# Ten shared-expert tiles lead instead of eight, TensorE adds the expert rows of six token tiles in PSUM, and ten tiles' gated results are prepared between routed tiles

## The chip, the cores and the metric

The kernel runs on one core of a Trainium2 chip. The metric is the device time of one execution in microseconds. The engines are TensorE (PE; its weight loads are PEld), VectorE (DVE), ScalarE (ACT), GpSimd (POOL) and SyncE (SP), which here only issues transfers.

## The reference

One transformer block over x of 8 batches x 256 tokens x 256 values, fp32, with adaptive layer norm. `sa, ca, ga, sb, cb, gb` are six rows per batch from a small product of the condition.

```python
h = layernorm(x) * (1 + ca) + sa
x = x + ga * attention(h)        # 8 heads, 2 kv heads, window of 64, softcap 30
h = layernorm(x) * (1 + cb) + sb
x = x + gb * moe(h)
# moe: 16 experts, each token goes to 4 of them (from 2 of 4 groups), weights normalised
y = sum over the token's 4 experts of weight * ((silu(h @ w1[e]) * (h @ w3[e])) @ w2[e])
z = (silu(h @ sw1) * (h @ sw3)) @ sw2          # two shared experts of 176
moe = y + z
```

The change concerns only the last line of the block, x + gb * (y + z), and the order in which z and y are computed.

## The kernel before, in words

**Tiles and units.** The 2048 tokens are 16 token tiles of 128. After attention, every token's row (256 values, its weights and its target ids) is sent by GpSimd to the slots of its four experts in device memory (`rows_d`, 64 indirect transfers). The expert part is a list of 96 jobs: shared tiles 0 to 7, then 80 routed tiles of 128 slots each (16 experts, partly padded), then shared tiles 8 to 15. A shared tile is two units (two shared experts), a routed tile one: 112 units, numbered from 0; routed units are 16 to 95. `FIRST` is the number of shared tiles that lead.

**Steps.** Each engine has its own written order, one function `step(u)` per unit. In step u, TensorE transposes the rows of the tile that starts with unit u+2, multiplies unit u up (`up_mm`, L1640 to L1642, from fp32 split into a high and a low part, three products each), turns the hidden rows of unit u-2 and multiplies unit u-3 down (L1662 to L1666) into one of two PSUM banks for results (`y_bank`). ScalarE makes high parts and silu, and in step u evacuates the result of the job that ended with unit u-4: for a shared tile into `hrow` (L1452, over the tile's own input, so it waits until the tile's rows are sent), for a routed tile into `yout` (L1456), from where GpSimd sends the rows to `y_d`, four rows to a token (L1422). VectorE makes low parts (L1548, L1577) and the product of silu and up part (`hidden`, L1570, L1573). The low part of expert n's weights is split off by VectorE in unit `HIGH_AT[n] + 1` (L234, L241), every second unit.

**The first ten steps** of the expert part are woven by hand into the end of attention and routing (`drain`). There the last rows are sent and the table of routed tiles is worked out; SyncE then issues the loads of slot rows (`xin`, L1402), six tiles ahead, each released by the `hidden` of six tiles before.

**The tail.** SyncE issues behind the last `xin` the eight rows `gb` (one for each batch, spread over 128 partitions, L1406), waits until all of `y_d` is written, and loads for each token tile its four rows per token (`yt`, 512 KB, L1411) and x1, the block's x before the experts (`x1t`, four tiles at a time, L1413). GpSimd adds the four rows in two operations for each of 16 tiles (L1426, L1428). VectorE's `combine(t)` adds the shared result in `hrow` (L1486), multiplies by gb (L1489), adds x1 (L1492); SyncE stores the tile (L1388). `combine(0)` stands in step 103, one more in each step behind it, the last three behind the steps.

## Time and profile before

| | us |
|---|---|
| median of 3 runs | 536.2 (529.27 to 537.77) |
| profiled execution | 530.26 |
| its span | 528.4 |
| TensorE busy | 412.7 |
| VectorE busy | 384.7 |
| GpSimd busy | 259.2 |
| ScalarE busy | 243.5 |
| moved by DMA | 69.69 MB, mean 132 GB/s |

The span is the time from the first to the last instruction of the profiled execution; 1.9 us lie around it. Busy times are sums over stretches with different work: attention up to about 250 us, routed tiles from 299.5 to 472, the tail behind them. A row of the timeline gives start and length of an instruction, or of several alike, and in brackets how long its engine had been idle and what released it. "issue" is a wait for nothing that the profile shows; "remote" is one whose releaser is not among the core's own recorded events.

### The profile page before, as it was taken

The page shows a single profiled execution, that of the slowest core. Times are in us where ns is not written, and L with a number is a line of the kernel's source. Part 1 is how long each engine was busy: PE and PEld are TensorE (multiplying, and loading weights), DVE is VectorE, ACT ScalarE, POOL GpSimd, SP SyncE. Part 2 cuts the span into 40 slices and gives each one's busy share as a digit, 9 for nine tenths or more (in the row PEclk, how much of TensorE's full clock was granted, in tenths as well). Part 3 has the DMA queues.
Part 4 walks back from the last instruction along what each step waited for, and adds up shares of the span by engine and source line. Part 5 has one row for each costly group of instructions (what it writes and reads, how often), then busy time and mean ns, then how long its engine had stood idle before and what let it go on. Part 6 is the DMA issues. An engine that isn't in the chain of part 4 may idle for free.

```text
span 528.4 us, 10590 instructions
## 1 busy us (share of the span) xinstructions
PE 412.7 (78%) x2841; PEld 376.0 (71%) x2841; DVE 384.7 (73%) x1175; ACT 243.5 (46%) x569; POOL 259.2 (49%) x262
## 2 busy tenths in 40 slices
PE   3758869778967666097834999999999999998543
PEld 3447768676856554096734988999999999988532
DVE  2698796986867773228756889877777777747997
ACT  3446647434461501123322777566666666644210
POOL 1294262434867577404374026544545444446990
PEclk9855997877998855559795999999999999999875
DMA  8422313301230309202352636444444444639932
GB/s 304 154 70 88 96 37 108 99 0 62 66 110 20 122 31 334 88 0 86 128 222 72 205 101 198 139 140 147 139 142 139 138 143 139 152 103 345 396 125 90
DMA packets 38712, 69.69 MB, mean 132 GB/s; under 512 B 5753, under 2 KB 27897, under 8 KB 38657
## 3 DMA queue, kind: packets, MB, share of 16 engines
q1 hardware_dynamic: 30736, 45.51, 27.2%
q0 software_dynamic: 6912, 19.93, 10.2%
q10 hardware_dynamic: 1008, 3.57, 2.2%
q8 instruction: 27, 0.44, 0.4%
q14 instruction: 29, 0.23, 0.1%
HBM read 42.49 MB, written 26.51 MB: 131 GB/s over the span
## 4 chain that ended last, share of the span: by engine, by line
PE 46%; DVE 23%; issue 10%; another core or an unknown queue 6%; POOL 6%; ACT 5%; DMA 3%; DVEq 0%; SPq 0%; ACTq 0%; POOLq 0%
PE sc_ps L1640 5%; PE sc_ps L1642 5%; PE sc_ps L1641 5%; PE qkv_ps L1623 3%; POOL rn L449 3%; DVE yt L1486 2%; DVE yt L1489 2%; PE qkv_ps L912 2%; PE pv L1003 2%; PE pv L1004 2%; PE pv L1001 2%; DMA y_d<-yout,to 1%; PE qkv_ps L914 1%; PE qkv_ps L913 1%
## 5 line engine op out<-in xcount | busy, mean ns | idle before, releaser
L1422 POOL DMA_INDIRECT y_d<-yout,to x80 | 81.2, 1015 | 108.8 <-ACT yout L1456 102.3
L1291 POOL DMA_INDIRECT rows_d<-hrow,slots x64 | 67.5, 1054 | 36.9 <-issue 16.8
L449 POOL TENSOR_TENSOR rn<-meansq,minus_half 128x12 f32<-128x12 f32 x16 | 36.7, 2306 | 64.4 <-DVE meansq L710 64.4
L1570 DVE SCALAR_TENSOR_TENSOR hid<-silu,xin,sc_ps 128x64 f32<-128x64 f32 (+1 forms) x160 | 47.2, 336 | 20.5 <-PE tp L1651 7.2
L1435 ACT ACTIVATE f_xh<-qkv_ps 128x256 fp32r<-128x256 f32 x96 | 36.9, 384 | 52.2 <-PE qkv_ps L1623 42.4
L1640 PE MATMUL sc_ps<-w_routed,f_xh 128*128 x160 | 58.3, 365 | 0.0
L1440 ACT ACTIVATE silu<-sc_ps 128x176 f32<-128x176 f32 x112 | 35.7, 319 | 47.7 <-PE sc_ps L1642 40.2
L1642 PE MATMUL sc_ps<-w_routed,f_xh 128*128 x160 | 51.7, 323 | 0.0
L1641 PE MATMUL sc_ps<-w_routed,f_xl 128*128 x160 | 51.6, 323 | 0.0
L1548 DVE TENSOR_TENSOR f_xl<-qkv_ps,f_xh 128x256 fp32r<-128x256 f32 x96 | 40.6, 423 | 12.0 <-ACT f_xh L1435 7.5
L1623 PE MATMUL qkv_ps<-ident,xin 128*128 128x128 f32 x160 | 30.6, 273 | 0.2 <-DMA xin<-rows_d 0.2
L1640 PEld LDWEIGHTS sc_ps<-w_routed,f_xh 128*128 128x128 f32 x160 | 30.2, 189 | 0.5 <-issue 0.2
L1641 PEld LDWEIGHTS sc_ps<-w_routed,f_xl 128*128 128x128 f32 x160 | 30.4, 190 | 0.0
L973 PE MATMUL sc_ps<-mask,ident_b 128*128 128x320 bf16 x64 | 15.7, 384 | 18.4 <-ACT capped L551 18.1
L1642 PEld LDWEIGHTS sc_ps<-w_routed,f_xh 128*128 128x128 f32 x160 | 30.0, 188 | 0.0
L551 ACT ACTIVATE capped<-sc_ps 128x1280 f32<-128x1280 f32 x16 | 19.8, 1240 | 21.8 <-remote 16.7
L1003 PE MATMUL pv<-v,probs 128*128 128x33 f32 x128 | 27.6, 300 | 0.0
L1004 PE MATMUL pv<-v,probs 128*128 128x33 f32 x128 | 27.6, 300 | 0.0
L1573 DVE TENSOR_TENSOR hid<-silu,sc_ps 128x64 f32<-128x64 f32 x64 | 14.8, 272 | 16.9 <-ACT silu L1440 10.7
L1445 ACT ACTIVATE f_hth<-sc_ps 128x256 fp32r<-128x256 f32 x59 | 22.8, 387 | 8.8 <-PE sc_ps L1651 3.4
L1426 POOL TENSOR_TENSOR yt<-yt 128x512 f32<-128x512 f32 x16 | 22.1, 1380 | 5.8 <-DMA yt<-y_d 5.8
L1577 DVE TENSOR_TENSOR f_htl<-sc_ps,f_hth 128x256 fp32r<-128x256 f32 x59 | 24.6, 417 | 0.0
(261 smaller groups left out, 1371.1 us busy)
## 6 DMA issues: line engine op xcount, KB each, us to landing
xin<-rows_d SPq DMA_DIRECT2D x80, 144.0 KB
yt<-y_d SPq DMA_DIRECT2D x16, 512.0 KB, 11.6
raw<-in_w_raw SPq DMA_DIRECT2D x9, 608.0 KB
mod<-mod_rows SPq DMA_DIRECT2D x8, 384.0 KB
w_stage<-in_w_raw SPq DMA_DIRECT2D x4, 608.0 KB
raw<-in_w_raw ACTq DMA_DIRECT2D x4, 608.0 KB
rows_d<-zeros SPq DMA_DIRECT2D x16, 144.0 KB
x1d<-x SPq DMA_DIRECT2D x8, 256.0 KB
```

What stands on the lines that cost most here:

```text
L449: pool.tensor_tensor(rn[:, part], meansq[:, part], minus_half[:, part], ALU.pow).then_inc(s.rn_done, 1)
L1003: pe.matmul(o[:, 1, j], probs[:, g, j, 2 * P:3 * P], v[:, p, 0, g], start=True, stop=False, skip_group_check=True)
L1004: mm = pe.matmul(o[:, 1, j], probs[:, g, j, 0:P], v[:, p, 1, g], start=False, stop=True, skip_group_check=True)
L1291: pool.indirect_dma_start(rows_d, bass.IndirectOffsetOnAxis(ap=r.slots[:, t, k:k + 1], axis=0), hrow[:, t], None).then_inc(r.sent[t // QT] ...
L1422: pool.indirect_dma_start(y_d, bass.IndirectOffsetOnAxis(ap=to[:, i:i + 1], axis=0), yout[:, i % YR], None)\
L1435: act.activation(xh[:, j % XB], xt_ps[:], ACT.Copy).then_inc(s.xh, 1)
L1548: dve.tensor_tensor(xl[:, j % XB], xt_ps[:], xh[:, j % XB].bitcast(F32), ALU.subtract).then_inc(s.xl, 1)
L1570: dve.scalar_tensor_tensor(out=hid[:, u % HB3, to_cols], in0=silu[:, u % 2, cols], scalar=weight, in1=y, op0=ALU.mult, op1=ALU.mult).then_ ...
L1623: mm = pe.transpose(xt_ps[:, c], src[:, c * P:(c + 1) * P], ident[:])
L1640: pe.matmul(o, xh[:, j % XB, c], wh, start=(c == 0), stop=False)
L1641: pe.matmul(o, xl[:, j % XB, c], wh, start=False, stop=False)
L1642: mm = pe.matmul(o, xh[:, j % XB, c], wl, start=False, stop=(c == KC - 1))
```

## The change

- `FIRST` is 10: units 0 to 19 are shared, 20 to 99 routed, 100 to 111 shared. The weight splits of experts 7 to 17 stand at unit 10, 12, ... instead of 8, 10, ...
- For the six token tiles 10 to 15, ScalarE no longer evacuates the shared result and GpSimd no longer adds rows. The result stays in PSUM (three banks in turn), and TensorE adds the token's four rows to it, by four products with the identity (`add_rows`, step of the tile's last unit + 5). VectorE's `combine` then has two operations: times gb (read from PSUM), plus x1.
- For the ten leading tiles, `base(t)` runs between routed tiles, in step 42 + 4t: `hrow` = shared result times gb, plus x1, two VectorE operations. x1 comes through one buffer of a tile (`x1b`), its load issued by SyncE ahead of the `xin` load number 24 + 4t. `combine` has two operations here as well: the four rows' sum times gb, plus `hrow`.
- The `gb` rows are loaded ahead of the `xin` load number 20.
- The `yt` loads and the stores follow the order in which VectorE combines: 10, 11, 0, 1, 12, 2, 3, 13, 4, 5, 14, 6, 7, 15, 8, 9, from step 106 to step 117. For tiles 10 to 15 x1 follows each `yt` load.

```diff
-FIRST = 8
+FIRST = 10
-HIGH_AT = {n: 8 + 2 * (n - EARLY) for n in range(EARLY, NE)}
+HIGH_AT = {n: 10 + 2 * (n - EARLY) for n in range(EARLY, NE)}
-            for u in range(10, f.units + 3):
+            for u in range(10, f.units + 5):
...
-    results = [sc_ps[:, 3], qkv_ps[:, 1]]
+    results = [sc_ps[:, 3], qkv_ps[:, 1], pv[:]]
...
     def y_bank(j):
+        if j >= FIRST + TILES:
+            return (j - FIRST - TILES) % 3
         return (j - TWO_Y) % 2 if j >= TWO_Y else 0
...
+    x1b = w.raw[:].rearrange("p a n -> p (a n)")[:, B * HID:(B + 1) * HID]
+    GATES_AT = 20
+    LOAD_X1_AT = {GATES_AT + 4 + 4 * t: t for t in range(FIRST)}
+    BASE_AT = {SHARED * FIRST + i - 2: t for i, t in LOAD_X1_AT.items()}
...
-    COMBINE_AT = SHARED * FIRST + TILES + 7
+    COMBINE_AT = SHARED * FIRST + TILES + 8
+    PUT = {}
+    for t in range(FIRST, NT):
+        PUT.setdefault(last[TILES + t] + 5, []).append(t)
+    for t in range(FIRST):
+        PUT.setdefault(COMBINE_AT + t, []).append(t)
+    ORDER = [t for u in sorted(PUT) for t in PUT[u]]
...
         for i in range(TILES):
             if i >= XR:
                 sp.wait_ge(s.hid, first[FIRST + i - XR] + 1)
+            if i == GATES_AT:
+                for n in (NE - 2, NE - 1):
+                    split_done(sp, w, n)
+                for b in range(B):
+                    sp.dma_start(gb[:, b], mod_rows[b:b + 1, 3].to_broadcast([P, HID])).then_inc(gb_in, 16)
+            if i in LOAD_X1_AT:
+                t = LOAD_X1_AT[i]
+                after(sp, s.based, 2 * t)
+                sp.dma_start(x1b, x1d[t]).then_inc(x1_in, 16)
...
-        for n in (NE - 2, NE - 1):
-            split_done(sp, w, n)
-        for b in range(B):
-            sp.dma_start(gb[:, b], mod_rows[b:b + 1, 3].to_broadcast([P, HID])).then_inc(gb_in, 16)
...
-        for t in range(NT):
+        for t in ORDER:
             rows = y_d[t * P * TOPK:(t + 1) * P * TOPK].rearrange("(p k) h -> p (k h)", k=TOPK)
             sp.dma_start(yt[:, t], rows).then_inc(yt_in[t], 16)
-            if t % 4 == 0:
-                sp.dma_start(x1t[:, t:t + 4], x1d[t:t + 4].rearrange("t p h -> p t h")).then_inc(x1_in[t // 4], 16)
+            if t >= FIRST:
+                sp.dma_start(x1t[:, t], x1d[t]).then_inc(yt_in[t], 16)
...
-        for t in range(NT):
+        for t in range(FIRST):
             pool.wait_ge(yt_in[t], 16)
...
-            if ends(u - 4):
+            if ends(u - 4) and units[u - 4][0] < FIRST + TILES:
                 evacuate(units[u - 4][0])
...
+    def base(dve, t):
+        dve.wait_ge(s.evac, t + 1)
+        dve.wait_ge(gb_in, 16 * B)
+        dve.tensor_tensor(hrow[:, t, 0:HID], hrow[:, t, 0:HID], gb[:, t // QT], ALU.mult).then_inc(s.based, 1)
+        dve.wait_ge(s.based, 2 * t + 1)
+        dve.wait_ge(x1_in, 16 * (t + 1))
+        dve.tensor_tensor(hrow[:, t, 0:HID], hrow[:, t, 0:HID], x1b, ALU.add).then_inc(s.based, 1)
...
     def combine(dve, t):
+        if t < FIRST:
+            dve.wait_ge(s.added2, t + 1)
+            dve.tensor_tensor(yt[:, t, HID:2 * HID], yt[:, t, 0:HID], gb[:, t // QT], ALU.mult).then_inc(s.based, 1)
+            dve.wait_ge(s.based, 2 * FIRST + t + 1)
+            dve.tensor_tensor(x1t[:, t], yt[:, t, HID:2 * HID], hrow[:, t, 0:HID], ALU.add).then_inc(s.stored, 1)
+        else:
+            dve.wait_ge(s.total, t - FIRST + 1)
+            dve.wait_ge(gb_in, 16 * B)
+            dve.tensor_tensor(yt[:, t, HID:2 * HID], results[y_bank(TILES + t)][:, 0:HID], gb[:, t // QT], ALU.mult).then_inc(s.taken, 1)
+            dve.wait_ge(s.taken, t - FIRST + 1)
+            dve.tensor_tensor(x1t[:, t], yt[:, t, HID:2 * HID], x1t[:, t], ALU.add).then_inc(s.stored, 1)
...
             if 0 <= u - 2 < N:
                 low(u - 2)
+            if u in BASE_AT:
+                base(dve, BASE_AT[u])
+            for t in PUT.get(u, []):
+                combine(dve, t)
...
+        def add_rows(t):
+            pe.wait_ge(yt_in[t], 32)
+            o = results[y_bank(TILES + t)][:, 0:HID]
+            for k in range(TOPK):
+                mm = pe.matmul(o, ident[:], yt[:, t, k * HID:(k + 1) * HID], start=False, stop=(k == TOPK - 1))
+            mm.then_inc(s.total, 1)
...
             if 0 <= u - 3 < N:
                 down_mm(u - 3)
+            if ends(u - 5) and units[u - 5][0] >= FIRST + TILES:
+                add_rows(units[u - 5][0] - TILES)
```

## Rows read from the trace of the kernel before

**Rows 1.** Page, part 1: busy time, share of the span, instructions.

```profile
PE 412.7 (78%) x2841; PEld 376.0 (71%) x2841; DVE 384.7 (73%) x1175; ACT 243.5 (46%) x569; POOL 259.2 (49%) x262
```

**Rows 2.** Busy time (count) by stretch, granted clock, DMA share, GB/s.

```profile
299.51:336.89 37.38, 35.05 (x243) 31.95 (x242) 33.35 (x98) 26.06 (x69) 15.68 (x12) 1.00 0.46 138
336.89:463.01 126.12, 126.12 (x946) 124.79 (x945) 94.63 (x314) 78.70 (x249) 59.76 (x63) 1.00 0.48 142
...
482.00:515.40 33.40, 19.27 (x111) 16.62 (x109) 32.85 (x52) 8.11 (x24) 32.11 (x30) 0.84 0.76 287
515.40:528.43 13.03, 4.46 (x17) 3.74 (x17) 10.35 (x27) 1.15 (x3) 0.08 (x1) 0.50 0.26 91
```

**Rows 3.** Who ended TensorE's waits, 262 to 290: total, times, longest.

```profile
PE sc_ps L1662 <- ACT hrow L1452: 12.3, 1, 12.3
```

**Rows 4.** Timeline: start, us, engine, line, [idle before <-releaser], 273 to 296.

```profile
273.73 0.32 ACT L1440 ACTIVATE silu<-sc_ps 128x176 f32<-128x176 f32 x1 [4.37 <-remote]
...
283.63 0.38 ACT L1452 ACTIVATE hrow<-sc_ps 128x256 f32<-128x256 f32 x1 [6.67 <-remote]
...
289.24 30.67 SPq L1402 DMA_DIRECT2D xin<-rows_d  x14
...
295.38 0.38 PE L1623 MATMUL qkv_ps<-ident,xin 128*128 128x128 f32 x2
```

**Rows 5.** Timeline where routed tiles end and loads begin, 472 to 484.

```profile
472.21 0.29 PE L1666 MATMUL sc_ps<-w_routed,f_htl 128*128 x1
...
475.67 0.32 SPq L1411 DMA_DIRECT2D yt<-y_d  x1
...
479.39 1.29 POOL L1426 TENSOR_TENSOR yt<-yt 128x512 f32<-128x512 f32 x1 [5.21 <-DMA yt<-y_d]
...
482.11 1.56 POOL L1426 TENSOR_TENSOR yt<-yt 128x512 f32<-128x512 f32 x1 [0.61 <-DMA yt<-y_d]
```

**Rows 6.** Timeline: a shared unit, a weight split, the gate rows' loads.

```profile
291.75 0.41 PE L1640 MATMUL sc_ps<-w_shared,f_xh 128*128 128x352 f32 x1
...
312.13 1.15 DVE L234 TENSOR_TENSOR w_routed<-raw,w_routed 128x960 fp32r<-128x960 f32 x1
313.31 0.42 DVE L241 TENSOR_TENSOR w_routed<-raw,w_routed 64x256 fp32r<-64x256 f32 x1
...
454.38 3.67 SPq L1406 DMA_DIRECT2D raw<-mod_rows  x8
```

**Rows 7.** Who ended ScalarE's waits, 455 to 475.

```profile
ACT yout L1456 <- DMA y_d<-yout,to: 3.4, 2, 2.2
```

**Rows 8.** Two transfers in the chain that ended last: start, us.

```profile
314.93 5.67 DMA xin<-rows_d
...
458.36 7.61 DMA y_d<-yout,to
```

**Rows 9.** By line, busy us, mean ns: VectorE 482 to 515.4, GpSimd's tail.

```profile
L1492 DVE TENSOR_TENSOR x1t<-yt,x1t 128x256 f32<-128x256 f32 x8 | 10.5, 1308 | 0.3
L1486 DVE TENSOR_TENSOR yt<-yt,hrow 128x256 f32<-128x256 f32 x8 | 9.0, 1131 | 0.0
L1489 DVE TENSOR_TENSOR yt<-yt,raw 128x256 f32<-128x256 f32 x8 | 7.3, 909 | 0.3
...
L1577 DVE TENSOR_TENSOR f_htl<-tp,f_hth 128x256 fp32r<-128x256 f32 x5 | 2.1, 413 | 0.0
...
L1426 POOL TENSOR_TENSOR yt<-yt 128x512 f32<-128x512 f32 x16 | 22.1, 1380 | 5.8 <-DMA yt<-y_d 5.8
L1428 POOL TENSOR_TENSOR yt<-yt 128x256 f32<-128x256 f32 x16 | 12.7, 793 | 1.3
```

**Rows 10.** Groups by line, VectorE behind 515.4.

```profile
L1489 DVE TENSOR_TENSOR yt<-yt,raw 128x256 f32<-128x256 f32 x8 | 3.4, 425 | 0.3
```

**Rows 11.** Timeline: the widest full fp32 products in the trace.

```profile
17.45 3.60 PE L1046 MATMUL sc_ps<-probs,ct_silu 128*8 128x512 f32 x8
```

**Rows 12.** Timeline: the last operation of a computing engine.

```profile
525.87 0.43 DVE L1492 TENSOR_TENSOR x1t<-yt,x1t 128x256 f32<-128x256 f32 x1
```

More of the change, by code:

```diff
@@ L1361, in experts @@
     s = named({n: sem("f_" + n) for n in (
-        "xt xh xl up silu hid dup ht hth htl down evac to summed stored added1 added2 gated spread").split()})
+        "xt xh xl up silu hid dup ht hth htl down evac to total taken based stored added1 added2 spread").split()})
     x_in = [sem(f"f_x_in{j}") for j in range(XR)]
@@ L1384, in ends, with store @@
         return 0 <= u < N and last[units[u][0]] == u
-    def store(sp, c):
-        sp.wait_ge(s.stored, c + 1)
-        sp.dma_start(out[c], x1t[:, c]).then_inc(out_sent, 16)
+    def store(sp, n, t):
+        sp.wait_ge(s.stored, n + 1)
+        sp.dma_start(out[t], x1t[:, t]).then_inc(out_sent, 16)
     def sync(sp):
@@ L1480, in scalar @@
         return step
-    def combine(dve, t):
-        dve.wait_ge(s.added2, t + 1)
-        total = yt[:, t, 0:HID]
-        dve.wait_ge(s.evac, FIRST if t < FIRST else TILES + t + 1)
-        dve.tensor_tensor(total, total, hrow[:, t, 0:HID], ALU.add).then_inc(s.summed, 1)
-        dve.wait_ge(s.summed, t + 1)
-        dve.wait_ge(gb_in, 16 * B)
-        dve.tensor_tensor(yt[:, t, HID:2 * HID], total, gb[:, t // QT], ALU.mult).then_inc(s.gated, 1)
-        dve.wait_ge(s.gated, t + 1)
-        dve.wait_ge(x1_in[t // 4], 16)
-        dve.tensor_tensor(x1t[:, t], yt[:, t, HID:2 * HID], x1t[:, t], ALU.add).then_inc(s.stored, 1)
+    def base(dve, t):
[5 more added lines that the diff above has]
+        dve.tensor_tensor(hrow[:, t, 0:HID], hrow[:, t, 0:HID], x1b, ALU.add).then_inc(s.based, 1)
+    def combine(dve, t):
+        if t < FIRST:
[9 more added lines that the diff above has]
+            dve.tensor_tensor(x1t[:, t], yt[:, t, HID:2 * HID], x1t[:, t], ALU.add).then_inc(s.stored, 1)
     def finish(dve):
-        for t in range(N + 4 - COMBINE_AT, NT):
-            combine(dve, t)
+        for u in range(N + 4, max(PUT) + 1):
+            for t in PUT.get(u, []):
+                combine(dve, t)
     def place_last(dve):
@@ L1591, in step @@
                 low(u - 2)
-            if 0 <= u - COMBINE_AT < NT:
-                combine(dve, u - COMBINE_AT)
+            if u in BASE_AT:
+                base(dve, BASE_AT[u])
+            for t in PUT.get(u, []):
+                combine(dve, t)
         return step
@@ L1659, in down_mm @@
             if begin:
-                after(pe, s.evac, same_before(y_bank, j))
+                before = same_before(y_bank, j)
+                after(pe, s.evac, min(before, FIRST + TILES))
+                after(pe, s.taken, before - FIRST - TILES)
             o = results[y_bank(j)][:, 0:HID]
@@ L1665, in down_mm @@
             pe.matmul(o, hth[:, q, 1], at(P, O2B, RAW), start=False, stop=False)
-            pe.matmul(o, htl[:, q, 1], at(P, O2B, RAW), start=False, stop=end).then_inc(s.down, 1)
+            pe.matmul(o, htl[:, q, 1], at(P, O2B, RAW), start=False, stop=end and j < FIRST + TILES).then_inc(s.down, 1)
+        def add_rows(t):
[4 more added lines that the diff above has]
+            mm.then_inc(s.total, 1)
         def step(u):
```

6 lines of the change are left out of this document (3 added, 3 removed).

## The prediction, made before the changed kernel ran

> **What bounds the kernel now.** I read the head of the page first, then busy time by stretches, then who ended TensorE's waits, then the order of instructions at the two joints. TensorE is the busiest engine, but its share is an average of very different stretches [rows 1]. While the routed tiles run, it is never idle: 63 units (946 pieces, 15 to a unit) in 126.12 us, 2.00 each. After 482 us VectorE is the full one (32.85 of 33.40 us) and GpSimd runs beside it without a pause, while TensorE drops to 58% and in the last 13 us to the lower clock [rows 2]. So the change has two sides: what it does to the time at which the routed tiles end, and what it does to the tail behind them.
>
> There is a third place. Before the routed tiles TensorE stands for 12.3 us until a ScalarE copy at 283.63. ScalarE itself was waiting, three times in a row (the first and the last are shown), for something that the trace calls remote [rows 3, 4]. I can't name the cause. GpSimd is sending rows all through this stretch, and nothing up to shared unit 9 is changed but a weight split that moves from unit 8 to unit 10. So I keep the wait as it is. The first rows load only at 289.24, and TensorE turns the first routed tile at 295.38, when they are barely there [rows 4]: the eight leading tiles already fill the time until then.
>
> **The routed tiles end later.** Call T0 the issue of the first load of gathered rows, 475.67. It follows the last routed unit's down product (472.21) by a fixed chain: ScalarE's copy, GpSimd's send, its landing [rows 5].
> - Two more tiles lead: four units. Shared units 12 to 15 took from 291.75 to 299.51, where the first routed unit starts, 1.94 each [rows 2, 6]: **+7.8**. Nothing covers them, since TensorE works without a gap from there on.
> - Weight splits. The 16 routed units from 299.51 to 336.89 took 37.38 where 16 x 2.00 is 32.0 [rows 2]. They hold seven splits (1.15 + 0.42 of VectorE each [rows 6]), so a split among routed units costs 0.76, and among shared units nothing, as 1.94 shows. With splits two units and tiles two units later, one more falls among shared units: **-0.8**. The weights stay ahead of their tiles (split 17 at unit 31, used at unit 35).
> - `base`: ten times two VectorE operations of 0.42 [rows 10], 0.87 in one unit of four. VectorE does 94.63 us in 63 units, 1.50 of every 2.00 [rows 2]. A split (1.57) exceeds the spare of two units (1.0) by 0.6 and costs 0.76; `base` doesn't exceed it. Between 0 and 0.16 x 10 = 1.6: **+0.5**. Its x1 load is issued four units (8.0 us) ahead of its use; rows loads on the same queue, with the same lead, cost nothing in the steady stretch.
> - The gate rows' eight loads move from behind the last rows load to ahead of the 21st. Their issue takes 3.67 us and today delays the sends of results, for which ScalarE waits 3.4 us [rows 6, 7]. That price moves along. New is that rows loads stand behind them: 3.67 + a landing of up to 7.61 [rows 8] is 11.3 against 8.0 of lead, so 0 to 3.3. One MB at the 0.4 MB/us of the tail is 2.5, and with about 2.4 of latency the sum is 8.6: **+0.8** with a little delay of results beside it.
> - Third result bank, order of stores, fewer ScalarE copies (six of 0.38 less [rows 4]): 0. ScalarE is busy 8.11 of 33.40 us in the tail [rows 2].
>
> T0 moves by 7.8 - 0.8 + 0.5 + 0.8 = **+8.3**, to 484.0.
>
> **The tail, from T0.** Today it is 528.43 - 475.67 = 52.8 us. GpSimd adds 16 tiles at 1.38 + 0.79 = 2.2 us from 479.39 on [rows 5, 9]. VectorE's three combining operations read two SBUF operands and take 1.31, 1.13 and 0.91 beside GpSimd, against 0.42 when it has stopped [rows 9, 10]. The difference that reads PSUM keeps its 0.41 in the same stretch [rows 9]. So: an operation from two SBUF operands costs 1.1 beside GpSimd, one with a PSUM operand 0.4. All of today's tail is 24 of the first kind, the unit work, and eight combines at the end.
>
> The Trainium skill ("SBUF — State Buffer", section Who interferes with whom) states the same split by operands and that the pair of ports is held for the whole instruction. By that, an operation arriving at random would wait half of a GpSimd operation, about 0.55, and take 0.97 instead of 1.1: the tail would be about 1 us shorter. The rows decide for 1.1.
>
> After the change:
> - Loads. Today the first half MB is used 3.7 us after T0 and the second load, behind 1.5 MB, after 6.4 [rows 5]: 2.4 us and then 0.4 MB/us. New order 10, 11, 0, 1, 12, 2, 3, 13, 4, 5, 14, 6, 7, 15, 8, 9, with x1 rows behind 10 to 15: tile 10 is there at +3.9, tile 0 at +6.8, tile 9 at +25 to +28.
> - GpSimd: ten tiles from +6.8 at 2.2 are done at +29, at the latest +29.7.
> - TensorE. Unit 103 starts 3.3 before T0, as unit 99 does today right behind the down product at 472.21 [rows 5]; a unit takes 1.9. Adding a tile's rows is four full fp32 products of 256 columns. The nearest row is four products of 512 columns that stand as eight pieces, 3.60 us together [rows 11]; half the columns make 1.8 us at the full clock, up to 3.6 at the lower one.
> - VectorE, in its written order. Tile 10: rows added by TensorE at +6.0, stored +6.9. Unit 108 and tiles 11 and 0: TensorE's sum +11.9, VectorE 0.4 + 1.1 + 2.2, to +15.6. Unit 109, tile 1: +18.8. Unit 110, tiles 12 and 2: +23.3. Unit 111, tile 3: +26.5. Tiles 13 and 4: +30.2; GpSimd has stopped. Last difference and tile 5: +31.5. TensorE now does the last down product, the rows of 14 (+33.2) and of 15 (+34.9); VectorE follows with 14, 6, 7, 15, 8, 9 at 0.9 each: **+38.6**. The last store adds 2.1, as today (525.87 + 0.43 against 528.43 [rows 12]): +40.7. For rows that TensorE adds at the lower clock, which it has today in the last 13 us [rows 2], I add 0.8 of the possible 2.3: **41.5**.
>
> The tail loses 52.8 - 41.5 = 11.3, the front gives back 8.3: **-3.0 us**. The profiled execution took 530.3 (span 528.4 and 1.9 around it), so 527.3 of that kind. The median of the runs shown, 536.2, lies 5.9 above the profiled one; with the same difference the changed kernel stands at **533**.
>
> **The rivals.**
> 1. *The tail is bound by GpSimd's ten tiles alone.* If VectorE and TensorE keep up, the end is T0 + 29.7 + 0.9 + 2.1 = 32.7, and the whole -11.8 (524). For: VectorE has 12 + 20 combining operations instead of 48. Against: five operations of 1.1 and 2.4 us of unit work per two units are 7.9, against the 3.8 of TensorE's two units. Chance 0.12.
> 2. *The two tiles cost little in front,* because the 12.3 us wait is shorter in other executions or under this order. Without it unit 10 could start at about 274 and the first routed tile would stand waiting for rows until 295; two more tiles would fill that. The front would then give back some 2 and the total be -9 (527), up to -12. Against: the wait is in the execution that is the second fastest of four. Chance 0.12.
> 3. *Slower: `base` waits for its x1 rows.* The wait stands on VectorE between a difference and the next unit's product, so all of the pipeline stands behind it. It decides once the load takes over 8.0 us. A rows load took 5.67 and a send of results beside the gate loads 7.61 [rows 8]. To reach +2% (10.7 us) the ten must cost (10.7 + 3.0) / 10 = 1.4 each, a landing of 9.4; at 10 us the total is +17 (553). Against: in the steady stretch no rows load was late. Chance 0.06.
> 4. *The tail does not shorten,* since VectorE ends up waiting for TensorE, which waits for loads and for VectorE in turn, at the lower clock: sums of 3.6 us put the last of them 5 to 8 us later, and the total is +2 to +5 (540). Chance 0.12.
>
> **How the numbers follow.** The forecast has 0.58, its own range -9 to +2. A measurement of this kernel can tell about 2% (10.7 us) from no change. Faster by more: most of rival 1, some of rival 2, a corner of the forecast: 0.22. Slower by more: rival 3 and a corner of 4: 0.08. Same: 0.70. The runs before spread from 529.3 to 537.8 by themselves; with the bounds of 1 (-12) and 4 (+5) around 533 the range is 522 to 541.
>
> **What would show it.** Right: unit 99 at the place where unit 95 was plus 8; first load of rows at about 484; two-operand operations of 1.1 until GpSimd stops about 29 us later, PSUM-reading multiplications of 0.4; eight pieces of 1.8 us per tile on TensorE. Wrong: no 12 us wait ahead of unit 9's products; idle VectorE in the tail; VectorE waiting for x1 in the routed stretch; TensorE's rows waiting for a load.

## The result

The changed kernel takes **541.9 us** (median of six runs, 537.1 to 546.1), the kernel before 536.9 in the same comparison (six runs, 529.3 to 629.8). Some executions of either kernel are slower than the rest, and the ratios and their 95% intervals, here and below, are worked out without them. The ratio is 1.0136 (1.0087 to 1.0186): about 7 us slower, under the 2% that a measurement of this kernel can tell from no change. The prediction was 533, its range 522 to 541.

The profiled execution took 546.1 us and has a span of 543.2. First the busy times, which answer to [rows 1], then the same stretches of both kernels. In a row of windows stand the stretch, its length, and then for each engine busy time and count; behind them are the granted clock, the DMA share and GB/s.

The kernel after, page, part 1:

```profile
PE 431.2 (79%) x2889; PEld 388.8 (72%) x2889; DVE 376.3 (69%) x1179; ACT 243.0 (45%) x563; POOL 245.5 (45%) x250
```

The kernel before: the first 23 routed units, the next 47, and the last routed and first shared units up to the start of unit 99:

```profile
299.51:350.91 51.40, 49.07 (x348) 45.83 (x347) 43.95 (x133) 34.91 (x97) 22.33 (x19) 1.00 0.46 139
350.91:445.11 94.20, 94.20 (x708) 93.20 (x707) 70.76 (x236) 59.37 (x188) 44.90 (x48) 1.00 0.46 141
445.11:472.33 27.22, 25.98 (x192) 25.25 (x191) 17.72 (x61) 15.52 (x50) 12.43 (x14) 1.00 0.50 135
```

The kernel after: the same units (numbers four higher), and the tail from the start of unit 103, which answers to the last two of [rows 2]:

```profile
313.83:371.37 57.54, 50.75 (x348) 48.18 (x347) 42.27 (x131) 34.04 (x96) 21.45 (x19) 0.94 0.46 139
371.37:472.87 101.50, 101.24 (x709) 93.31 (x707) 76.60 (x256) 60.66 (x188) 45.62 (x48) 1.00 0.47 144
472.87:498.34 25.47, 25.47 (x192) 25.20 (x190) 17.64 (x61) 15.87 (x50) 12.26 (x14) 1.00 0.31 98
498.34:543.20 44.86, 30.18 (x192) 27.66 (x190) 30.50 (x66) 7.74 (x24) 22.66 (x22) 0.94 0.70 258
```

Unit 10 starts at 286.4 before and at 293.9 after; of what was changed only the place of one weight split lies ahead of it, and 6.1 of the 7.5 us are there at unit 0 already, so I set them aside. From there on:

| | before | after | difference | predicted |
|---|---|---|---|---|
| unit 10 to the first routed unit | 13.1 | 19.9 | +6.8 | +7.8 |
| 23 routed units | 51.4 | 57.5 | **+6.1** | 0 (gate loads +0.8, a split -0.8) |
| the next 47 | 94.2 | 101.5 | **+7.3** | +0.5 |
| up to unit 99 (103) | 27.2 | 25.5 | -1.8 | 0 |
| from there to the end | 56.1 | 44.9 | -11.2 | -11.3 |

From unit 10 to the end that is +7.3 us, as much as the ratio says. The match is no proof of the parts: the two profiled executions lie 15.8 us apart (546.1 and 530.3), and half of that is the 7.5 us ahead of unit 10. The tail came out as forecast, the two more tiles nearly so. The loss lies in two stretches that I had priced at next to nothing. The -1.8 belongs to the gate loads too: they have left that place. With these loads behind the last rows load the stretch takes 26.1 to 27.2 us (e4, e2 and the kernel before), in all fifteen profiles with them ahead of it 25.5.

**The first 23 routed units.** Timeline of the kernel after around them: SyncE's issues, GpSimd's sends of results, and TensorE.

```profile
344.35 2.71 SPq L1426 DMA_DIRECT2D xin<-rows_d  x2
348.37 5.21 SPq L1419 DMA_DIRECT2D raw<-mod_rows  x8
...
353.26 0.96 POOL L1442 DMA_INDIRECT y_d<-yout,to  x1 [1.04 <-ACT yout L1476]
354.07 3.08 SPq L1426 DMA_DIRECT2D xin<-rows_d  x4
...
358.67 0.69 PE L1655 MATMUL qkv_ps<-ident,xin 128*128 128x128 f32 x2 [4.61 <-DMA xin<-rows_d]
359.09 0.65 PE L1672 MATMUL sc_ps<-w_routed,f_xh 128*128 x1
...
360.33 0.96 POOL L1442 DMA_INDIRECT y_d<-yout,to  x1 [6.11 <-ACT yout L1476]
```

The eight gate rows' loads hold the queue for 5.2 us and bring 1 MB ahead of the next rows. TensorE stands 4.6 us for them, and its next products run at the lower clock (L1672 takes 0.65 there and 0.42 at the full clock, below; the granted clock of the whole stretch is 0.94). The three units around it took 7.05, 3.69 and 2.58 instead of 2.0 each: +7.3.

**The next 47.** No wait of TensorE stands in this stretch: it counts as busy for 101.24 of 101.50 us, yet does the same 47 units as before in 94.20. The cause is seen only in the order of instructions. VectorE, then TensorE, around one `base`:

```profile
388.71 0.42 DVE L1607 TENSOR_TENSOR f_htl<-sc_ps,f_hth 128x256 fp32r<-128x256 f32 x1
389.05 0.41 DVE L1505 TENSOR_TENSOR hrow<-hrow,raw 128x256 f32<-128x256 f32 x1
389.50 0.42 DVE L1508 TENSOR_TENSOR hrow<-hrow,raw 128x256 f32<-128x256 f32 x1
389.84 0.42 DVE L1578 TENSOR_TENSOR f_xl<-qkv_ps,f_xh 128x256 fp32r<-128x256 f32 x1
...
390.40 0.41 PE L1655 MATMUL qkv_ps<-ident,xin 128*128 128x128 f32 x2
390.84 0.42 PE L1672 MATMUL sc_ps<-w_routed,f_xh 128*128 x1
```

`f_xl` (L1578) is the difference that frees the one PSUM bank of turned rows. In a unit without `base` ahead of it, it starts 0.7 us after the unit's first product; here it starts 1.34 us after it (the unit's first product was at 388.50). TensorE turns the next rows (L1655) only behind it, and the next unit starts after 2.34 instead of 2.00. That is +0.34 for a `base`, and the unit behind it is late too (2.15).

### The profile page after: what moved, and what is told of

The parts are those of the page before. It is cut to its first block, busy times and chain, and to the rows that moved or that the text cites. A ratio compares the mean times of both kernels' runs of the same rounds, so it can differ in the third digit from the quotient of the medians.

```text
span 543.2 us, 10664 instructions
## 1 busy us (share of the span) xinstructions
PE 431.2 (79%) x2889; PEld 388.8 (72%) x2889; DVE 376.3 (69%) x1179; ACT 243.0 (45%) x563; POOL 245.5 (45%) x250
## 4 chain that ended last, share of the span: by engine, by line
PE 55%; DVE 15%; issue 10%; another core or an unknown queue 6%; ACT 5%; POOL 4%; DMA 2%; SPq 1%; DVEq 0%; ACTq 0%
PE sc_ps L1672 6%; PE sc_ps L1674 5%; PE sc_ps L1673 5%; PE qkv_ps L1655 4%; POOL rn L449 3%; PE qkv_ps L912 2%; PE sc_ps L1696 2%; PE sc_ps L973 1%; PE qkv_ps L913 1%; PE qkv_ps L914 1%; PE pv L1004 1%; PE pv L1003 1%; PE pv L1001 1%; PE qkv_ps L1696 1%
## 5 line engine op out<-in xcount | busy, mean ns | idle before, releaser
L1600 DVE SCALAR_TENSOR_TENSOR hid<-silu,xin,sc_ps 128x64 f32<-128x64 f32 (+1 forms) x160 | 47.1, 335 | 24.5 <-issue 11.2
L1455 ACT ACTIVATE f_xh<-qkv_ps 128x256 fp32r<-128x256 f32 x96 | 36.8, 384 | 58.2 <-PE qkv_ps L1655 36.2
L1672 PE MATMUL sc_ps<-w_routed,f_xh 128*128 x160 | 59.5, 372 | 0.3
L1578 DVE TENSOR_TENSOR f_xl<-qkv_ps,f_xh 128x256 fp32r<-128x256 f32 x96 | 40.6, 423 | 21.2 <-ACT f_xh L1455 18.4
L1674 PE MATMUL sc_ps<-w_routed,f_xh 128*128 x160 | 52.2, 326 | 0.0
L1655 PE MATMUL qkv_ps<-ident,xin 128*128 128x128 f32 x160 | 31.2, 277 | 4.6 <-DMA xin<-rows_d 4.6
L1672 PEld LDWEIGHTS sc_ps<-w_routed,f_xh 128*128 128x128 f32 x160 | 30.6, 191 | 2.7 <-issue 1.8
L973 PE MATMUL sc_ps<-mask,ident_b 128*128 128x320 bf16 x64 | 16.3, 395 | 19.8 <-ACT capped L551 19.1
L1004 PE MATMUL pv<-v,probs 128*128 128x33 f32 x128 | 28.5, 308 | 0.0
L1003 PE MATMUL pv<-v,probs 128*128 128x33 f32 x128 | 28.5, 308 | 0.0
L1603 DVE TENSOR_TENSOR hid<-silu,sc_ps 128x64 f32<-128x64 f32 x64 | 14.9, 274 | 19.0 <-ACT silu L1460 12.6
L973 PEld LDWEIGHTS sc_ps<-mask,ident_b 128*128 128x128 bf16 x64 | 7.3, 126 | 25.2 <-ACT capped L551 21.4
```

The lines of the kernel that those rows point to most:

```text
L1003: pe.matmul(o[:, 1, j], probs[:, g, j, 2 * P:3 * P], v[:, p, 0, g], start=True, stop=False, skip_group_check=True)
L1455: act.activation(xh[:, j % XB], xt_ps[:], ACT.Copy).then_inc(s.xh, 1)
L1578: dve.tensor_tensor(xl[:, j % XB], xt_ps[:], xh[:, j % XB].bitcast(F32), ALU.subtract).then_inc(s.xl, 1)
L1600: dve.scalar_tensor_tensor(out=hid[:, u % HB3, to_cols], in0=silu[:, u % 2, cols], scalar=weight, in1=y, op0=ALU.mult, op1=ALU.mult).then_ ...
L1655: mm = pe.transpose(xt_ps[:, c], src[:, c * P:(c + 1) * P], ident[:])
L1672: pe.matmul(o, xh[:, j % XB, c], wh, start=(c == 0), stop=False)
```

## The experiments

Sixteen runs on four chips, four on each. The number of the first chip, that of the result above, is not on record; I call it another one because of what follows. On these four the kernel before takes 513 to 515 us (medians) instead of 537, and two waits of TensorE for ScalarE are gone that both kernels showed on the first chip. TensorE's waits, total, times, longest, in the kernel before on the first chip, and then in the changed kernel on another (run e5):

```profile
PE sc_ps L973 <- ACT capped L551: 18.1, 7, 14.9
```

```profile
PE sc_ps L973 <- ACT capped L551: 4.1, 8, 1.4
```

The other wait is the one of [rows 3], 12.3 us before and 13.8 after. Neither is in any of the sixteen, nor any other wait of ScalarE for something "remote". So times are compared within a chip, as ratios to the kernel before run beside them, and stretches by the length of the same units. The stretches are the better evidence. In the sixteen profiles unit 0 starts anywhere between 215.7 and 228.4 us, although nothing ahead of it differs between these kernels, so that a whole time moves by 10 us and more for reasons that have nothing to do with the change.

**Theories.** A: the gate loads cost some 7 us because they come in one burst ahead of the rows loads. D: `base` costs some 7 because two operations in a row delay `f_xl`. X: it's the x1 loads, or VectorE's total work. Q: TensorE's sequencer, which executes several waits and a register load for each unit (its register load, L1635, takes longer in slow units), is the bound of a routed unit. C: the price of the two leading tiles depends on the 12 us wait.

### e1: gate loads spread

```diff
-            if i == GATES_AT:
-                ... all eight gb loads
+            if 0 <= i - (GATES_AT - 3) < B:
+                one gb load, b = i - (GATES_AT - 3)
```

> The changed kernel with the eight gate-row loads issued one each ahead of rows loads 17 to 24 instead of all eight ahead of the 21st. Theory A (rows loads queued behind eight bunched loads): the 7.05 and 3.69 us of units 38 and 39 fall to about 2.0 each, the sends of results are no longer delayed, and the time is 7 to 9 us under the changed kernel (about 534 where it is 542). Rival B (the price of the gate rows is the moving of 1 MB beside the results, wherever it stands): 0 to 2 us less, the lost time spread over units 35 to 42. The 7 us lost between units 43 and 90 stay in both.

Measured: ratio 0.9859 (0.9773 to 0.9944). Windows of e1, 23 and 47 routed units:

```profile
279.09:329.22 50.13, 48.20 (x349) 45.81 (x346) 42.59 (x131) 34.02 (x96) 21.45 (x19) 1.00 0.54 160
329.22:430.20 100.98, 100.63 (x709) 93.55 (x707) 76.39 (x256) 60.30 (x188) 45.67 (x48) 1.00 0.48 144
```

57.5 has become 50.1, with the same bytes on the same queue, and the clock stays at the upper level (1.00 instead of 0.94). The second stretch is as slow as before. A holds. The changed kernel did not run on this chip; beside its 0.998 on two others (e5, e13) the ratio is about 6 us better.

### e2: no base between routed tiles

The x1 rows are loaded in the tail and `combine` gets a third operation for tiles 0 to 9; the gate loads stand behind the last rows load again.

> The changed kernel without its preparation between routed tiles: gate rows loaded behind the last rows load as before, x1 of all tiles loaded in the tail, three operations in the combine of the ten leading tiles. Theory: the routed stretch is that of the kernel before (2.00 a unit, no loss at unit 38), which gives back 8 + 7 us less the 1.5 that the gate rows cost as before; the tail pays ten operations of 0.4 to 1.1 us and 1.3 MB more of loads, 4 to 10 us. Net 3 to 9 us under the changed kernel, about 536. If what slows the routed stretch is the third result bank or the leading tiles and not the preparation, the stretch stays slow and the time is 4 to 10 us over the changed kernel.

Measured: ratio 0.9865 (0.9611 to 1.0119). The interval is wide, since the ratio rests on two runs of this kernel. Windows of e2, the 47 units and the tail:

```profile
336.39:430.59 94.20, 94.20 (x708) 93.20 (x707) 70.65 (x236) 59.38 (x188) 44.78 (x48) 1.00 0.47 141
457.08:505.70 48.62, 33.53 (x192) 30.19 (x190) 35.38 (x76) 7.74 (x24) 22.28 (x22) 0.91 0.72 265
```

The 47 units take 94.20 to the hundredth, as in the kernel before. `base` and what comes with it cost the 7 us; without it the tail is 4.7 longer than in e1 (43.92).

### e3, e4: fewer waits on TensorE's sequencer

```diff
-                n = min(jobs[j][1], E - 1) + SHARED + 1
-                if n > EARLY:
+                n = jobs[j][1] + SHARED + 1
+                if EARLY < n <= NE:
```

From the seventeenth routed tile on this leaves out four waits per unit that were met long before; e3 is the changed kernel with it, e4 the kernel before.

> The changed kernel, with TensorE no longer repeating, for routed tiles 16 to 79, the four semaphore waits on weight splits that tile 15 has already passed. Theory Q (TensorE's instruction sequencer, not its array, sets the 2.00 us of a routed unit, and goes to 2.17 where its register load takes 0.48 instead of 0.30): four waits of 0.12 less take the sequencer under the array's time, a unit falls to 1.86 to 1.90 as for shared tiles, all of the loss between units 43 and 90 goes, and the time is 12 to 16 us under the changed kernel. Rival R (VectorE's two operations and their x1 load hold up the units in which they stand): units stay at 2.0 to 2.2, and the time is within 2 us of the changed kernel.

> The kernel before with the same four waits of TensorE left out for routed tiles 16 to 79. Theory Q: its 2.00 us a unit were the sequencer's as well; units 33 to 95 fall to 1.86 to 1.90 and the time by 6 to 9 us. If the 2.00 are the array's or VectorE's, nothing changes (within 1 us).

Measured: e3 1.0039 (0.9963 to 1.0116), e4 0.9994 (0.9921 to 1.0066). The 47 units: e3 96.48 us (below), e4 94.20. Q is wrong as put: no routed unit fell under 2.00 in either. But with `base` in place the sequencer's work matters, since the stretch lost 4 to 5 us of its excess: the unit behind a `base` takes 2.13 instead of 2.34, and most of those after it 2.00. The ratio doesn't show this gain (1.0039, where the changed kernel itself has 0.998 on other chips), so it rests on the stretch alone.

```profile
340.45:436.93 96.48, 96.41 (x709) 93.41 (x707) 75.81 (x256) 59.73 (x188) 45.52 (x48) 1.00 0.50 150
```

### e5: the changed kernel on another chip

> The changed kernel once more, beside the others of this call, because the chip of the last call showed no 12 us wait ahead of unit 9's products (5 to 6 us instead) and the kernel before stood waiting for rows at its unit 13 (7.8 us). Theory A (the gate rows' loads ahead of the 21st rows cost about 7 us, and base about 6 us): it stands 7 to 9 us above the kernel with spread gate loads, so at 1.000 to 1.006 of the kernel before on such a chip, with units 38 to 40 long (7, 3.7, 2.6 us) and routed units 43 to 90 at 2.15 on average. Rival (both were accidents of one execution): 0.985 of the kernel before, as with spread gate loads.

Measured: ratio 0.9983 (0.9931 to 1.0035). Both losses are there (57.55 and 100.83 us for the two stretches), but on this chip the change as a whole costs nothing. The kernel before has another wait in such an execution. TensorE's waits from 260 to 295 in e4, whose front is that of the kernel before:

```profile
PE qkv_ps L1623 <- DMA xin<-rows_d: 5.6, 1, 5.6
```

With no 12 us wait ahead, eight leading tiles end before the first rows have come. This is the mechanism of the prediction's second rival.

### e6, e7, e9: where base stands, and its loads

e6 cuts `base` in two and puts the parts behind `f_xl`, in two units; e9 puts both behind `f_xl` of one unit; e7 leaves `base` where it was and loads x1 once (nine tiles then add the wrong x1 rows). All have spread gate loads.

```diff
         def step(u):
             if starts(u + 2):
                 low_x(units[u + 2][0])
             ...
+            if u in BASE_AT:
+                base(dve, BASE_AT[u])            # e9: both operations
+            if u - 1 in BASE_AT:
+                base_x1(dve, BASE_AT[u - 1])     # e6: the addition, one unit later
             if 0 <= u < N:
                 hidden(u)
             ...
-            if u in BASE_AT:
-                base(dve, BASE_AT[u])
```

> Gate loads spread, and base cut in two: its multiplication stands on VectorE behind the difference that frees the bank of turned rows, and its addition at the same place one unit later, instead of both between two units. Theory D (two operations in a row, 0.85 us, push that difference from 0.7 to 1.3 us after the unit's start; TensorE's sequencer waits for it 0.5 us longer, and its following waits and register loads then run late for many units): each of the two now fits beside the wait for silu; units 43 to 90 take 2.00 each, 94 to 95 us for 47 of them instead of 100 to 101, and the time is 5 to 7 us less than with spread gate loads alone (about 0.973 of the kernel before). Rival X (the x1 rows' loads or VectorE's total work cost it, wherever base stands): within 2 us of the kernel with spread gate loads.

> Gate loads spread, base's twenty VectorE operations left where the change put them, but the x1 rows loaded only once, for tile 0; the nine other loads and their places on the queue are left out, so nine tiles add the wrong x1 rows. Theory D: the operations cost it, so nothing changes: units 43 to 90 at 2.13 to 2.15, the time within 1.5 us of the kernel with spread gate loads alone. Rival X (the loads and their waits): units 43 to 90 at 2.00, 5 to 7 us less.

> Gate loads spread; base's two operations stay together in one unit, but stand behind the difference that frees the bank of turned rows instead of ahead of it. Theory D in its narrow form (what counts is that this difference is not pushed): units 43 to 90 at 2.00 to 2.02, 94 to 95 us for 47, as with base split. Its wider form (0.85 us in one unit are too many wherever they stand, because the gated product then comes late for TensorE's turn of the next unit): units with base keep at least 0.2 us more, 47 units take 97 us or more.

Measured: e6 0.9746 (0.9634 to 0.9858), e7 0.9891 (0.9816 to 0.9966), e9 0.9892 (0.9800 to 0.9984). The 47 units of e6, e7 and e9:

```profile
332.65:427.23 94.58, 94.58 (x708) 93.26 (x707) 75.93 (x255) 59.37 (x188) 47.03 (x48) 1.00 0.50 153
```

```profile
332.86:432.61 99.75, 99.42 (x708) 93.63 (x706) 75.96 (x256) 59.76 (x188) 45.43 (x48) 1.00 0.43 133
```

```profile
329.72:426.05 96.33, 96.18 (x708) 93.55 (x707) 77.02 (x256) 59.71 (x188) 45.89 (x48) 1.00 0.51 150
```

e6 and e7 have the same VectorE work (75.9 us), e7 has nine loads less, and its 47 units take 5.2 us more: neither the loads nor the work carry the price, and X falls in both its forms. e7 does stand 0.3 to 1.2 us below the other kernels with `base` in the same place (e14 100.0, e1 101.0), so that much may be the loads'.

e9 keeps 96.3, between what the two forms of D gave (at most 95, at least 97). Most of the price was the delay of `f_xl`. Whether the rest comes with two operations in one unit is not settled. The unit behind a `base` takes up to 2.13 in e9 where e6 has 2.00, but kernels with the split `base` vary by as much: 94.6 (e6), 94.8 (e16), 95.8 (e15), 96.5 (e10). What these have beyond 94.2 are single late units and one or two behind each. The longest, one of 2.6 to 3.0 us in each of e10, e15 and e16, hold a wait for rows, as here in e10:

```profile
384.48 0.44 PE L1661 MATMUL qkv_ps<-ident,xin 128*128 128x128 f32 x2 [0.59 <-DMA xin<-rows_d]
```

All three times the late rows load is the one issued 0.8 us behind an x1 load, and no such wait stands in the 47 units of the kernel before or of e2, which have no x1 loads there. So X may hold for these single units; it was not tried with the split `base`. The timeline of VectorE in e6 shows how a half fits:

```profile
347.38 0.42 DVE L1581 TENSOR_TENSOR f_xl<-qkv_ps,f_xh 128x256 fp32r<-128x256 f32 x1
347.72 0.42 DVE L1506 TENSOR_TENSOR hrow<-hrow,raw 128x256 f32<-128x256 f32 x1
348.06 0.15 DVE L1588 TENSOR_TENSOR to<-xin,tab_spare 128x1 int32<-128x1 int32 x1
348.39 0.59 DVE L1603 SCALAR_TENSOR_TENSOR hid<-silu,xin,sc_ps 128x64 f32<-128x64 f32 x2 [0.18 <-ACT silu L1461]
```

The gated product (L1603) still finds VectorE idle: the half lies in the time in which it waits for silu.

### e8, e11: eight leading tiles

`FIRST` is 8 and the splits start at unit 8; gate loads spread, base split, TensorE adds the rows of eight tiles. In e11 the gate loads start three rows loads later and x1 four.

> Gate loads spread and base split, but only eight shared tiles lead, as in the kernel before; TensorE then adds the rows of eight token tiles. It prices the two more leading tiles. Theory C (on a chip without the 12 us wait, the first rows come only some 6 us after TensorE could turn them, so that two more leading tiles, 7.8 us of units, cost about 2 in front): routed units end about 2 us earlier than with ten leading tiles and base split, the tail is longer by the two tiles' units less what they saved, and the time is within 3 us of it, on either side. Rival (they cost their full 7.8 in front): routed units end 8 us earlier, the time is 2 to 5 us less.

> Eight leading tiles, base split, and gate loads one by one from the 21st rows load on, x1 loads four units later: with eight leading tiles and the loads from the 18th on, the first gate load waited on the queue for the last weight split (units 30 to 32 took 4.8, 2.7, 2.9 us, some 6 us too much). Theory C (two more leading tiles cost only about 2 us in front where the first rows come late, and bring 3 to 5 in the tail): that loss is gone, 16th to 39th unit take about 51 us, and the time is within 2 us of ten leading tiles with base split, about 0.973 to 0.979 of the kernel before. Rival (the two tiles cost their 7.8 in front here too): 0.965 or less.

Measured: e8 0.9885 (0.9803 to 0.9967), e11 0.9807 (0.9685 to 0.9929). In e8 the 23 units took 55.6; by the order on the queue the first gate load waited there for a weight split, two units later relative to the rows than with ten leading tiles. So e8 prices nothing, and e11 moves the loads. Windows of e11: unit 10 to the first routed one, 23 units, 47 units, the tail from unit 99 on:

```profile
254.80:272.98 18.18, 14.34 (x88) 13.91 (x87) 11.53 (x33) 8.63 (x22) 5.35 (x5) 0.84 0.63 192
272.98:323.91 50.93, 48.98 (x348) 45.87 (x347) 43.50 (x133) 34.89 (x97) 22.29 (x19) 1.00 0.55 155
323.91:419.57 95.66, 95.55 (x708) 93.24 (x707) 74.79 (x252) 59.56 (x188) 46.54 (x48) 1.00 0.50 151
445.04:493.80 48.76, 41.73 (x264) 38.28 (x262) 31.24 (x80) 10.90 (x34) 18.29 (x18) 1.00 0.67 243
```

With ten leading tiles (e6) unit 10 to the first routed unit took 20.27: two more tiles cost 2.1 us in front by this pair. Other pairs give less: the stretch takes 18.2 to 20.8 us with eight leading tiles (e11, e8, e12, e4) and 19.1 to 20.3 with ten (the other twelve). So they cost between nothing and 2 us here, far from 7.8, as C says. The tail is 1 to 5 us shorter with them (43.5 to 46.8 with ten and `base`, 47.7 to 48.8 with eight and `base`). The times of e11 and e6 can't be told apart. The tail of 56 us before is 48.8 with as many leading tiles as before, so most of the gain is TensorE adding rows and `base`, not the two tiles.

### e10, e12: the small weight difference one unit later

```diff
                 if u == HIGH_AT[n] + 1:
                     split_low(dve, w, n)
-                    split_low_b(dve, w, n)
+                if u == HIGH_AT[n] + 2:
+                    split_low_b(dve, w, n)
```

e10 is e6 with it, e12 is e11 with it.

> Gate loads spread, base split, and the small one of a weight split's two VectorE differences (0.42 us) moved one unit behind the large one (1.15 us). Units 20 to 43 hold seven splits and take 50.2 us for 23 units, 46 at 2.00 each. Theory D carried over (what exceeds the spare time of one unit costs, so cutting helps): 0.2 to 0.4 us less for each of the seven, 47.5 to 49 us for the 23 units, 1.5 to 3 us off the time. Rival (the large one alone already sets the price, and the other unit now pays too): 50 us or more.

> The last one and the small difference of each weight split moved one unit later: the best combination if both hold. By theory D 1.5 to 3 us less than the kernel without that move; by its rival no less or more.

Measured: e10 0.9835 (0.9731 to 0.9939), e12 0.9798 (0.9666 to 0.9931). The 23 units of e10 took 49.47 instead of 50.18, those of e12 49.75 instead of 50.93: about a microsecond instead of 1.5 to 3, and nothing in the time. Here the large difference alone (1.15 us) sets the price; D, carried over, promised too much.

### e13 to e16: all on one chip

e13 is the changed kernel, e14 has the spread gate loads, e15 the split base too, and e16 also the fewer waits.

> The changed kernel, as the reference of this call. Theory A + D: units 20 to 43 in 57.5 us, units 43 to 90 in 101, the time 11 to 15 us above base split. Rival (their sum is not additive, for instance because another wait takes over): less than 8 us above it.

> Gate loads spread. Theory A + D: units 20 to 43 in 50.2 us, units 43 to 90 in 101 as before the repair, the time 6 to 8 us under the changed kernel of this call.

> Gate loads spread and base split. Theory A + D: units 20 to 43 in 50.2 us, 43 to 90 in 94.5, the time 5 to 7 us under the kernel with spread loads alone, 11 to 15 under the changed one, 0.97 to 0.98 of the kernel before (0.98 to 0.99 if this chip shows the 12 us wait ahead of unit 9's products, since the two leading tiles then cost 7.8 instead of 2).

> As the last, and TensorE's sequencer skips four waits per routed unit, from the seventeenth routed tile on, that were met long before. Theory S (these waits cost only where something has made the sequencer late; with base split nothing does): within 1.5 us of the kernel with base split, units 43 to 90 at 2.00. Rival Q (the sequencer's own work is the bound of a routed unit): units 43 to 90 under 1.97, 2 us or more off the time.

| | mean us | ratio to before | 23 units | 47 units | unit 0 to the end |
|---|---|---|---|---|---|
| e13 changed | 506.2 | 0.9984 (0.9771 to 1.0197) | 58.2 | 100.8 | 285.8 |
| e14 gate loads spread | 501.8 | 0.9898 (0.9703 to 1.0092) | 51.3 | 100.0 | 279.1 |
| e15 base split too | 499.0 | 0.9842 (0.9723 to 0.9961) | 50.2 | 95.8 | 274.6 |
| e16 fewer waits too | 495.7 | 0.9777 (0.9633 to 0.9921) | 50.1 | 94.8 | 276.5 |

The means are those of the runs behind the ratios, three to five of each kernel. They fall by 4.4 and 2.8 us with the two repairs, 7.2 together, which is what the rival promised (less than 8) and not A + D (11 to 15). The two stretches together fall by 7.6 and 5.4, 13.0 in sum, and from unit 0 to the end of the profile it is 6.7 and 4.5, 11.2 in sum (the end of the table; e4, in front and routed stretch the kernel before, has 286.6). The intervals of the ratios overlap widely. That the repairs add up is therefore shown for the stretches, and not for the whole time. e16's units stay at 2.00, as S says and Q doesn't; its mean is 3.3 us below e15's, more than S allows (1.5), but from unit 0 to the end it is 1.9 above it.

## Why the prediction was wrong

**"The gate rows' eight loads: +0.8"** failed first; it measured 7.3, and 5.5 net of the 1.8 that the loads no longer cost at their old place, a price that I had moved along. I had the right picture (issue plus landing against the lead), and the lead was wrong: 8.0 us, where it is 5.7. The rows load of a tile is released by the `hidden` of six tiles before, but that comes 2.3 us after the unit's first product, and TensorE turns the rows right ahead of the unit two before their own. The chain in e5, VectorE, SyncE and TensorE:

```profile
309.15 0.60 DVE hid L1600 x2
309.77 0.33 SPq L1419
...
314.03 5.69 DMA xin<-rows_d
...
319.76 0.69 PE qkv_ps L1655 x2
```

The rows load is issued 4.3 us after the first gate load and lands 5.7 later, together 10.0, less 5.7 of lead: TensorE waits 4.3, more than my upper bound of 3.3. The issue was not mis-sized. It took 3.8 here against the forecast 3.67 [rows 6], and the 5.21 in the changed kernel's first profile made no difference to the loss, since the landing was shorter there (4.6): the 23 units take 57.5 in both. There the wait is 4.6 of the 7.3 us, and the other 2.7 had no term at all: the unit behind the stop runs at the lower clock (3.69), and the next is late as well (2.58). e1 shows that the burst costs this, not the loads. One at a time they cost next to nothing: 50.1 us (e1), with one such run at 51.3 (e14), against 50.2 without them (e2).

**"`base`: between 0 and 1.6, +0.5"** failed second; it measured 7.3. The step compared VectorE's work with its idle share over two units (1.0 us) and found that 0.87 fits. VectorE's idle time, 0.5 us a unit, lies in pieces, and the place between `f_htl` and `f_xl` has hardly any (0.06 us in the kernel before, at 351.55). What counts is the one operation behind the insertion that TensorE waits for, `f_xl`, and its slack. e6 and e7, with the same busy time and 5 us apart, show it.

A late `f_xl` also costs more than its own delay. After each `base` the next unit is long as well, and behind the last one, from 449 to 473, eleven units without `base` still took 2.17 each. That they stay slow is not the rule: in e14, with `base` in the same place, the units are back at 2.00 from the fourth one on, while e1 stays slow like the changed kernel. In the slow units TensorE's sequencer needs longer for its register load of the expert's number. The kernel before (393 to 415), the changed one (449 to 473) and e6 (its 47 units); columns are count, ns min/median/max:

```profile
L1603 PEldq TENSOR_LOAD <-tab_expert x11: 298/300/309, 393.2 to 413.3; - x11
```

```profile
L1635 PEldq TENSOR_LOAD <-tab_expert x11: 300/500/548, 449.4 to 471.1; - x11
```

```profile
L1640 PEldq TENSOR_LOAD <-tab_expert x47: 296/301/392, 332.9 to 425.4; - x47
```

e3 shows that a sequencer with four waits less recovers within a unit or two, e16 that it sets no pace of its own once nothing has made it late. In the unit that starts at 461.92 its other instructions follow each other every 0.10 to 0.15 us without a pause, so that there a longer load makes the unit longer. Why the load takes 0.5 us there stays open: SyncE and VectorE load registers from such tables in every unit too, and whether these loads meet was not tried alone.

**"Two more tiles: +7.8"** was right for the chip of the prediction (+6.8), because the 12 us wait covers the arrival of the rows there. On the four chips without that wait they cost between nothing and 2. I had given this the second rival, at 0.12, on the ground that the wait was in the execution shown; but none of the sixteen on the four chips shows it, so it is not in the kernel; whether it goes with the chip or with the hour is not shown. The rival promised a total of -9 there; by the ratios it is -1 (e5, e13) with the two losses and -8 to -13 without them (e15, e6).

**The tail: -11.3**, measured -11.2, and from the first `yt` load to the end 41.5 as forecast, but by luck. These parts held roughly: GpSimd's first operation at T0 + 8.5 with T0 at 501.69 (forecast 6.8), its last ended at T0 + 32.0 (29), eight pieces of 1.9 us a tile on TensorE (1.8). VectorE ended at T0 + 35.9, not 38.6, and the last store landed at T0 + 37.7, 1.7 us after its issue. By the forecast's own path the kernel would have ended at T0 + 38.1.

What ended it at 41.5 is in none of my terms. GpSimd's sequencer closes the program with a DRAIN that starts with GpSimd's last addition and takes 10.06 us, and the last instructions of all other engines come behind its end. GpSimd's DRAIN in the kernel before, then after (ns min/median/max, start in us):

```profile
L256 POOLq DRAIN  x1: 10067/10067/10067, 514.6 to 514.6; - x1
```

```profile
L256 POOLq DRAIN  x1: 10063/10063/10063, 532.9 to 532.9; - x1
```

Before, it ended at 524.7, under VectorE's work, and the span ended 0.4 us behind the last landing. After, it ended at 543.0, 3.6 us behind the last landing. In eight of the eighteen profiles (after, e1, e5, e9, e10, e13, e14, e15) it ends last, in the other ten the end is 0.4 us behind the last landing. So the path of the first rival, GpSimd's additions, did set the end, only with a DRAIN behind them that the rival didn't have. No run moved GpSimd's last addition alone; by these rows (an estimate) up to 3.4 us of the tail were to be had by ending it earlier.

Lines of the tail after (busy us, mean ns):

```profile
L1513 DVE TENSOR_TENSOR yt<-yt,raw 128x256 f32<-128x256 f32 x10 | 8.0, 799 | 0.0
L1515 DVE TENSOR_TENSOR x1t<-yt,hrow 128x256 f32<-128x256 f32 x10 | 7.9, 790 | 0.3
L1519 DVE TENSOR_TENSOR yt<-qkv_ps,raw 128x256 f32<-128x256 f32 x2 | 0.8, 425 | 2.1 <-PE qkv_ps L1707 2.1
L1707 PE MATMUL qkv_ps<-yt,ident 128*128 128x256 f32 x16 | 3.8, 378 | 0.0
```

Operations on two SBUF operands took from 0.41 to 1.47 beside GpSimd, those that read PSUM 0.41 to 0.43 (L1519 is 425 ns with GpSimd running). The thirteen of L1513 and L1515 that started before GpSimd stopped average 1.0 us; with the five of L1521, which also read two SBUF operands, it is 0.89. The Trainium skill ("SBUF — State Buffer", section Who interferes with whom) gives the split by operands, and from it I had worked out 0.97 against the 1.1 that I took from the rows before: the rule's value was the nearer one.

Rivals: the first had the right path for the end and a wrong time, as said; the fourth (tail not shorter) did not happen. The third had the right place, VectorE between two units, and the wrong cause: no wait of VectorE for x1 stands in the 47 units, and without nine of the ten loads they are hardly faster (e7).

**The version to keep** is the change with spread gate loads and base split (e6, e15): 0.9746 (0.9634 to 0.9858, two runs) and 0.9842 (0.9723 to 0.9961, five runs) of the kernel before, against 0.9983 for the change as it was. Both intervals leave out 1 and neither lies wholly beyond 2%, so it is faster, by an amount that is open. Whether it also wins on a chip with the 12 us wait was not run; an estimate from the stretches is 1.0136 less 13 us of 537, near 0.99.

## What to carry to other kernels

- Work inserted on an engine in a locked pipeline is priced by the slack of the instruction behind it that another engine waits for, not by the engine's idle share. Cut it to the size of one gap and put it behind that instruction.
- Take the lead of a load from the timeline, from what releases it to what needs it (5.7 us here), and not from the count of units between the two (8.0).
- Look at how the program ends. An engine that finishes early can still have the last word, as GpSimd's 10 us here.
- Loads that nobody hurries for still cost when they come in a burst ahead of ones with a deadline: on a queue that serves a steady loop, issue them one per turn.
- Where a first-stage wait covers another (ScalarE's here covers the arrival of rows), a change's price in front depends on which of the two is there. Price it for both.

## What the runs showed of the hardware

- An engine can count as busy for all of a stretch and still be slower: TensorE 101.24 of 101.50 us for work that takes 94.20. Its matmuls' ends are modelled, so a late issue doesn't show as idle; the period of a unit does. The Trainium skill ("Perfetto Trace Analysis", section Sequencer-only Instruction) says that of an instruction which only the sequencer executes the profiler reports the execution and not the wait ahead of it. That fits the trace, which lists no wait of TensorE in the 101.5 us, but no run here tests it.
- One late unit can leave a rhythm that stays slow (2.17 instead of 2.00 for eleven units in the changed kernel, three units in e14), in which the sequencer's register load takes 500 instead of 300 ns.
- GpSimd's DRAIN at the end of the program took 10.0 to 10.07 us in all eighteen profiles; in eight of them it was what the program ended with.
- The same program differed by over 4% (537 against 513 to 515 us). TensorE's two waits for ScalarE, 15 and 12 us long and in the first two profiles only, are as large as that; ScalarE itself waits there for something that the trace calls remote. What that is, and whether it goes with the chip, is open.
